# A mixture-of-experts FFN kernel on one core: tile 2's expert mix moved from TensorE to ScalarE and VectorE, buffers and load order around it changed

## The reference, cut to what matters

```python
h = gelu(embedding @ W0 + b0); h = gelu(h @ W1 + b1)
att = softmax(h @ W2 + b2)                              # 32 x 8
agg_w = einsum('bk,koi->boi', att, weight)              # one 128x128 matrix per tile
y = einsum('boi,bih->boh', agg_w, x) + (att @ bias_k)[:, :, None]
# for gate and up, each with its own inv row: scale = max|y * inv| / 127 per row, q = round(y * inv / scale)
gate = (qg @ w_gate.T) * sg * s_wgate                   # 2048 -> 1024
up = (qu @ w_up.T) * su * s_wup
inter = clip(silu(gate) * up, -10, 10)
out = x + (qi @ w_down.T) * si * s_wdown                # quantised again, 1024 -> 2048
```

## Time and profile before

| what | value |
|---|---|
| time, median of 3 runs | 803.78 us (803.5 to 803.93) |
| profiled execution | 803.78 us |
| its span, first to last instruction | 802.0 us |
| around the span | 1.78 us |
| PE busy | 794.1 us (99%) |
| DVE, ACT, POOL busy | 715.4, 441.1, 147.9 us |
| stretch 9 to 56 us, PE idle | 0.47 us of 47 |

### The profile page before, as it was taken

One profiled execution on the slowest core, in us unless ns is written; L12 is line 12 of the kernel. 1 busy time (PEld: TensorE's weight loads), 2 busy tenths in 40 slices (PEclk: granted clock), 3 DMA queues, 4 the chain that ended last, 5 costly groups with the idle time before them and its releaser, 6 DMA issues.

```text
span 802.0 us, 9186 instructions
## 1 busy us (share of the span) xinstructions
PE 794.1 (99%) x3521; PEld 365.3 (46%) x3521; DVE 715.4 (89%) x810; ACT 441.1 (55%) x385; POOL 147.9 (18%) x138
## 2 busy tenths in 40 slices
PE   8999999999999999999999999999999999999997
PEld 5554444444444444444444444444444444444443
DVE  6897899999888998888998888998888988888968
ACT  7774335555664545664545654555654546655531
POOL 2703210210122220122220122210222210222000
PEclk9999999999999999999999999999999999999999
DMA  8998745454445444445444445445455444454342
GB/s 300 225 215 172 161 142 171 149 166 125 131 138 171 145 145 120 129 145 170 145 145 122 119 154 167 147 145 112 122 161 161 154 129 136 108 167 154 90 111 105
DMA packets 162964, 119.81 MB, mean 149 GB/s; under 512 B 151780, under 2 KB 152164, under 8 KB 153703
## 3 DMA queue, kind: packets, MB, share of 16 engines
q1 hardware_dynamic: 161192, 106.64, 44.6%
q0 software_dynamic: 1728, 12.58, 7.8%
HBM read 60.48 MB, written 33.55 MB: 117 GB/s over the span
## 4 chain that ended last, share of the span: by engine, by line
PE 88%; DVE 7%; ACT 2%; issue 1%; DMA 1%; DVEq 0%; ACTq 0%
PE gate_ps L613 26%; PE up_ps L613 25%; PE down_ps L716 22%; PE conv_ps L566 12%; DVE amax L1092 2%; PE gate_ps L716 1%; DVE region L1150 1%; DVE xt L1265 1%; DVE down_sc L1256 1%; ACT qg L820 0%; DMA qgT<-qg 0%; PE up_ps L566 0%; PE down_ps L571 0%; ACT y L809 0%; DVE region L1219 0%
## 5 line engine op out<-in xcount | busy, mean ns | idle before, releaser
L716 PE MATMUL down_ps<-wd,qiT 128*128 128x512 bf16 x896 | 211.2, 379 | 0.0
L613 PE MATMUL gate_ps<-wg,qgT 128*128 128x512 bf16 x928 | 205.7, 379 | 0.0
L613 PE MATMUL up_ps<-wu,quT 128*128 128x512 bf16 x896 | 202.4, 379 | 0.0
L1092 DVE TENSOR_REDUCE amax<-region 128x1 f32<-128x2048 f32 (+1 forms) x90 | 173.0, 1922 | 1.2
L442 POOL TENSOR_TENSOR prod<-wexp,att_bc 128x1024 f32<-128x1024 f32 x28 | 53.1, 1898 | 540.9 <-DVE region L1150 498.3
L716 PEld LDWEIGHTS down_ps<-wd,qiT 128*128 128x128 bf16 x896 | 87.6, 98 | 123.4 <-issue 28.5
L613 PEld LDWEIGHTS gate_ps<-wg,qgT 128*128 128x128 bf16 x928 | 90.8, 98 | 109.4 <-issue 1.1
L613 PEld LDWEIGHTS up_ps<-wu,quT 128*128 128x128 bf16 x896 | 87.7, 98 | 106.1 <-ACT quT L885 0.4
L820 ACT ACTIVATE qg<-region,recip 128x2048 f16<-128x2048 f32 x30 | 60.1, 2002 | 128.9 <-DVE recip L1102 128.9
L566 PE MATMUL conv_ps<-xt,aggw 128*128 128x512 f32 x244 | 116.9, 602 | 0.8 <-ACT y L809 0.5
L809 ACT ACTIVATE y<-conv_ps,aggb 128x512 bf16<-128x512 f32 x116 | 78.9, 686 | 59.6 <-PE conv_ps L566 55.0
(11 more groups left out here) (180 smaller groups left out, 582.1 us busy)
## 6 DMA issues: line engine op xcount, KB each, us to landing
xt<-x SPq DMA_DIRECT2D x30, 1024.0 KB, 4.8
out<-xt SPq DMA_DIRECT2D x29, 1024.0 KB, 4.0
wg<-w_gateT POOLq DMA_DIRECT2D x4, 1024.0 KB, 17.8
wu<-w_upT POOLq DMA_DIRECT2D x4, 1024.0 KB, 15.0
wd<-w_downT POOLq DMA_DIRECT2D x4, 1024.0 KB, 9.6
xt<-x SPq DMA_DIRECT2D x4, 512.0 KB, 4.8
invg_bc<-inv_gate SPq DMA_DIRECT2D x1, 1024.0 KB, 8.2
out<-xt SPq DMA_DIRECT2D x2, 512.0 KB, 2.9
```

The source lines that it names most:

```text
L613: last = nc.tensor.matmul(acc[:, n * BANK:(n + 1) * BANK], codes[:, k * P:(k + 1) * P], wts[:, k, n * BANK:(n + 1) * BANK], start=(k == 0) ...
L716: last = nc.tensor.matmul(down_bank(t, c), qiT_at(t)[:, k * P:(k + 1) * P], wd[:, k, c * BANK:(c + 1) * BANK], start=(k == ks[0]), stop=(k ...
L1092: nc.vector.tensor_reduce(amax[:, i:i + 1], src, axis=AX.X, op=ALU.max, apply_absolute_value=True).then_inc(max_ready, 1)
```

## The change

- Tile 2's mix leaves PE. `experts2` scales the eight experts on ACT, in four pieces between the chunks of `conv_out(0)`, into `prod2`, a part of `wu` that is still empty; `experts2_sum` adds them on DVE in three instructions, put in the middle of tile 0's maxima, into `aggw2`, a part of `qiT`. POOL's up weights wait for it. POOL now writes tile 3's diagonal instead of tile 2's, and `diagonals(3)` on DVE is gone.
- `conv(2)` moves ahead of `turn_g(0)`, `conv(3)` ahead of `turn_g(1)` and of `gate(1)`. Tile 3's `y` is written to `quT`, and its last two chunks use `up_ps`, which `gate(1)` uses too; so `gate(1)` waits for all of `conv_out(3)`.
- ACT's list is rearranged accordingly: `conv_out(2)` between the steps of tile 0, `conv_out(3)` ahead of `turned_g(1)`, `quant_g(2)` ahead of `quant_u(0)`.
- Tile 1's product for up goes to `XU_HOME` in `wd` instead of `region2`; DVE quantises `quant_g(2)` ahead of `quant_u(0)`; tile 3's gate product is made in two halves, one on each side of `gate_out(0)`.
- ACT's queue issues `b2` and `wexp`; SP's list is two issues shorter, and x of tile 3 no longer waits for gate weights. POOL issues the gate weights after x of tile 1 has landed, not x of tile 0.

```diff
...
-Y_HOME = [y[:, :], wd_part(0, bf16), wd_part(1, bf16)]
+Y_HOME = [y[:, :], wd_part(0, bf16), wd_part(1, bf16), quT[:, :]]
 XG_HOME = [region1[:, :], wd[:, :, :].rearrange("p k h -> p (k h)")[:, 6 * H:8 * H].bitcast(fp32)]
...
 def y_at(t):
-    return Y_HOME[t] if t < EARLY else y[:, :]
+    return Y_HOME[t] if t <= EARLY else y[:, :]
...
 def xu_at(t):
-    return XU_HOME if t in (2, EARLY) else region2[:, :]
+    return region2[:, :] if t == 0 or t > EARLY else XU_HOME
...
 ones = qiT[:, 0:2 * P].bitcast(fp32)
+aggw2 = qiT[:, 4 * P:6 * P].bitcast(fp32)
 filler = region1[:, 0:(P + BANK) // 2].bitcast(bf16)
...
 SPLIT = 5
-diag_at = [region2[:, I:H], prod_flat, region2[:, I:H], prod_flat]
+diag_at = {0: region2[:, I:H], EARLY: region2[:, I:H]}
+prod2 = wu[:, 4:6, :].rearrange("p k i -> p (k i)").bitcast(fp32).rearrange("p (k o) -> p k o", o=P)
...
 def conv_bank(t, c):
-    return bank(up_ps, c - 2) if t < EARLY and c >= 2 else bank(conv_ps, c % 2)
+    return bank(up_ps, c - 2) if t <= EARLY and c >= 2 else bank(conv_ps, c % 2)
...
+def aggw_at(t):
+    return aggw2 if t == 2 else aggw[t % 2][:, :]
+
 def xcols(t, c):
...
     sp.dma_start(mlp_s, mlp).then_inc(mlp_in, 16)
-    sp.dma_start(b2_s, b2.partition_broadcast(P)).then_inc(b2_in, 16)
-    sp.dma_start(wexp[:, :, :], weightT).then_inc(wexp_in, 16)
     sp.dma_start(xslot(0), x[0, :, :]).then_inc(x_in[0], 16)
...
         sp.dma_start(swd_s[i], rows[:, (5 + i) * I:(6 + i) * I]).then_inc(rows_in[2 + i], 16)
-    sp.wait_ge(wg_in[0], 16)
     sp.dma_start(xslot(3), x[3, :, :]).then_inc(x_in[3], 16)
...
     pool.wait_ge(att_dve, BIAS[0])
-    a = att_bc[:, 2 * K:3 * K].unsqueeze(2).to_broadcast([P, K, P])
-    nc.gpsimd.tensor_tensor(diag_at[2].rearrange("p (k r) -> p k r", r=P),
+    a = att_bc[:, EARLY * K:FIRST * K].unsqueeze(2).to_broadcast([P, K, P])
+    nc.gpsimd.tensor_tensor(diag_at[EARLY].rearrange("p (k r) -> p k r", r=P),
                             ident[:, :].unsqueeze(1).to_broadcast([P, K, P]), a, ALU.mult).then_inc(diag_pool, 1)
-    pool.wait_ge(x_in[0], 16)
+    pool.wait_ge(x_in[1], 16)
     for i in range(WCH):
...
     pool.wait_ge(row_spread, SWD)
+    pool.wait_ge(sum2, 3)
     for i in range(WCH - 1):
...
             pe.wait_ge(wexp_in, 16)
-        elif t == 2:
-            pe.wait_ge(diag_pool, 1)
         else:
-            pe.wait_ge(diag_dve, 1)
+            pe.wait_ge(diag_pool, 1)
         for k in ks:
...
                 pe.wait_ge(agg_sum, 1)
-            elif t < POOLED:
-                pe.wait_ge(agg_out, t - 1)
+            elif t == 2:
+                pe.wait_ge(sum2, 3)
+            elif t == EARLY:
+                pe.wait_ge(agg_out, 1)
             else:
...
                     pe.wait_ge(logits_out, 1)
-            elif t < EARLY or (t == EARLY and c < 2):
+            elif t <= EARLY:
                 pe.wait_ge(y_ready, NC * t + c - 3)
...
                 pe.wait_ge(y_ready, NC * t + c - 1)
-            nc.tensor.matmul(conv_bank(t, c), aggw[t % 2][:, :], xcols(t, c),
+            nc.tensor.matmul(conv_bank(t, c), aggw_at(t), xcols(t, c),
                              start=True, stop=True).then_inc(conv_done, 1)
...
                 pe.wait_ge(gcodes_ready, 1)
-                pe.wait_ge(agg_out, 2)
+                pe.wait_ge(agg_out, 1)
             turn(gturn_ps[:, h * I:(h + 1) * I], qg, KI, h * KI, gturn_mm)
...
                 pe.wait_ge(qgT_ready, t - EARLY)
-            if t == 0:
-                pe.wait_ge(agg_out, 1)
-            elif t == 1:
-                pe.wait_ge(y_ready, NC * EARLY)
+            if t == 1:
+                pe.wait_ge(y_ready, NC * FIRST)
             elif t == 2 or t == EARLY:
...
     conv(1)
-    aggregate_mm(2)
+    conv(2)
     turn_g(0, range(1))
-    aggregate_mm(3)
+    aggregate_mm(EARLY)
     gate(0, range(4))
     turn_g(0, range(1, 2))
-    conv(2)
+    conv(EARLY)
     turn_g(1)
...
     gate(1, HALVES[0])
-    conv(3)
     gate(0, range(8, 12))
...
                 act.wait_ge(att_dve, BIAS[0])
-            elif t == EARLY:
-                act.wait_ge(xg_ready, 1)
-                act.wait_ge(xu_ready, 1)
             elif t > EARLY:
...
             act.wait_ge(conv_done, NC * t + c + 1)
-            norm = erec[:, t:t + 1] if t < 2 else 1.0
+            norm = erec[:, t:t + 1] if t < EARLY else 1.0
             nc.scalar.activation(y_at(t)[:, c * BANK:(c + 1) * BANK], conv_bank(t, c), ACT.Identity,
...
+    def experts2(ks):
+        for k in ks:
+            nc.scalar.activation(prod2[:, k, :], wexp[:, k, :], ACT.Copy, scale=att_col(2, k)).then_inc(scaled2, 1)
+
     def experts(t):
...
     def aggregate_out(t):
-        act.wait_ge(agg_mm, t)
-        act.wait_ge(conv_done, NC * (t - 1))
+        act.wait_ge(agg_mm, 2)
+        act.wait_ge(conv_done, NC * 2)
         nc.scalar.activation(aggw[t % 2][:, :], agg_ps[t], ACT.Copy, scale=erec[:, t:t + 1]).then_inc(agg_out, 1)
...
             act.wait_ge(row_spread, INVI)
+        elif t == 2:
+            act.wait_ge(xu_ready, FIRST)
         for h in range(2):
...
+    act.dma_start(b2_s, b2.partition_broadcast(P)).then_inc(b2_in, 16)
+    act.dma_start(wexp[:, :, :], weightT).then_inc(wexp_in, 16)
     act.wait_ge(hid_mm, 1)
...
     nc.scalar.activation(group(logits, 1), log_ps[1], ACT.Copy).then_inc(logits_out, 1)
-    conv_out(0)
+    experts2(range(4))
+    conv_out(0, range(1))
+    experts2(range(4, 6))
+    conv_out(0, range(1, 2))
+    experts2(range(6, 7))
+    conv_out(0, range(2, NC))
+    experts2(range(7, K))
     conv_out(1)
+    conv_out(2, range(1))
     quant_g_first(0)
-    aggregate_out(2)
-    turned_g(0, range(1))
+    conv_out(2, range(1, 2))
     quant_g_first(1)
-    aggregate_out(3)
+    turned_g(0, range(1))
+    aggregate_out(EARLY)
+    conv_out(2, range(2, NC))
     turned_g(0, range(1, 2))
     quant_g(1)
-    conv_out(2, range(2))
-    turned_g(1, range(1))
-    conv_out(2, range(2, NC))
-    turned_g(1, range(1, 2))
-    quant_u(0)
-    conv_out(3)
+    conv_out(EARLY)
+    turned_g(1)
     quant_g(2)
+    quant_u(0)
     turned_g(2)
...
-    def diagonals(t):
-        dve.wait_ge(ident_set, 2)
-        dve.wait_ge(agg_sum, 1)
-        a = att_bc[:, t * K:(t + 1) * K].unsqueeze(2).to_broadcast([P, K, P])
-        nc.vector.tensor_tensor(diag_at[t].rearrange("p (k r) -> p k r", r=P),
-                                ident[:, :].unsqueeze(1).to_broadcast([P, K, P]), a, ALU.mult).then_inc(diag_dve, 1)
+    def experts2_sum():
+        dve.wait_ge(scaled2, K)
+        nc.vector.tensor_tensor(prod2[:, 0:4, :], prod2[:, 0:4, :], prod2[:, 4:8, :], ALU.add).then_inc(sum2, 1)
+        dve.wait_ge(sum2, 1)
+        nc.vector.tensor_tensor(prod2[:, 0:2, :], prod2[:, 0:2, :], prod2[:, 2:4, :], ALU.add).then_inc(sum2, 1)
+        dve.wait_ge(sum2, 2)
+        nc.vector.tensor_tensor(aggw2, prod2[:, 0, :], prod2[:, 1, :], ALU.add).then_inc(sum2, 1)
...
         dve.wait_ge(y_ready, NC * t + NC)
-        if t == 2 or t == EARLY:
-            dve.wait_ge(gcodes_ready, 1 if t == 2 else EARLY)
+        if t == 2:
+            dve.wait_ge(gcodes_ready, 1)
         elif t == EARLY + 1:
...
+    def xg_half(t, h):
+        cols = slice(h * I, (h + 1) * I)
+        if h == 0:
+            dve.wait_ge(y_ready, NC * t + NC)
+            dve.wait_ge(gcodes_ready, EARLY)
+        else:
+            dve.wait_ge(part_scaled, NC)
+        nc.vector.tensor_tensor(xg_at(t)[:, cols], y_at(t)[:, cols], invg_bc[:, cols],
+                                ALU.mult).then_inc(xg_ready if h else part_scaled, 1)
+
     def xg_scale(t):
...
             dve.wait_ge(agg_mm, 2)
-        elif t == 2:
+        elif t == 1:
             dve.wait_ge(gcodes_ready, 2)
...
                                     apply_absolute_value=True).then_inc(part_maxed, 1)
+            if c == 1:
+                experts2_sum()
         dve.wait_ge(part_maxed, NC)
...
     quant_first()
-    diagonals(3)
     quant_g(1)
-    quant_u(0)
     quant_g(2)
+    quant_u(0)
     quant_u(1)
-    xg_product(3)
+    xg_half(3, 0)
     gate_out(0)
+    xg_half(3, 1)
     xg_scale(3)```

On PE, from conv of tile 0 to the turn of tile 1; the transposes are the rows of 128x128 from `ident,qg`, the expert mix those from `wexp`. Before:

```order
L566 MATMUL conv_ps<-xt,aggw 128x512 x2
L566 MATMUL up_ps<-xt,aggw 128x512 x2
L566 MATMUL conv_ps<-xt,aggw 128x512 x2
L566 MATMUL up_ps<-xt,aggw 128x512 x2
L537 MATMUL gate_ps<-wexp,region 128x128 x8
L571 MATMUL down_ps<-ident,qg 128x128 x8
L537 MATMUL down_ps<-wexp,prod 128x128 x8
L613 MATMUL gate_ps<-wg,qgT 128x512 x8
L571 MATMUL down_ps<-ident,qg 128x128 x8
L566 MATMUL conv_ps<-xt,aggw 128x512 x2
L566 MATMUL up_ps<-xt,aggw 128x512 x2
L571 MATMUL down_ps<-ident,qg 128x128 x16
```

13 lines of the change are left out of this document (7 added, 6 removed).

## The result

The changed kernel takes 805.41 us in the median of 22 runs (804.80 to 806.86), the kernel before 803.81 us in 22 runs beside them (803.25 to 804.45). The ratio is 1.0020, with a 95% interval of 1.0014 to 1.0026, so 1.1 to 2.1 us slower. The prediction, 803.0 us in a range of 801.9 to 804.2, is wrong, and the sign with it. The profiled execution of the changed kernel took 805.66 us with a span of 803.9, against 802.0 before.

A forecast was written before the change was run, and what follows sets the result against it. PE was taken as the bound, with 88% of the chain. Mix 1.84 plus old waits 0.79, less new waits 0.46, 0.31, 0.34, 0.54 and loads 0.2, gave 0.78 us gain: 803.0 us, range 801.9 to 804.2.

The forecast's parts named there:

- the term on the loads: At the start, mlp shares with ACT's b2 and experts and lands 0 to 0.4 us later; 0.2 taken, all on the path.
- `mlp` at over 2.7 us: Sign at the start: mlp's transfer was expected at 2.3 to 2.7 us; longer would show the forecast wrong.
- Waits 1 to 4: New PE waits: tile 0's first turn 0.46 us, gate(0) 0.31, gate(1) 0.34, turn of tile 3 0.54.
- rival C: DVE's products block on POOL's row spreading, DVE's chain grows another 0.6 to 1.0 us: 803.8, no change; chance 0.12.
- A: Rival: ACT and DVE hand over faster, the first three new PE waits shrink to a third: 802.1; chance 0.13.
- B: Rival: first gate chunk, issued later and behind x of tile 3, lands at 25.7, gate(0) 1.25 us late: 804.2; chance 0.10.
- waits 1 to 3: New PE waits before tile 0's first turn (0.46 us), gate(0) (0.31) and gate(1) (0.34).
- what I don't see in the start: Chance of 0.05 for unforeseen effects at the kernel's start, half of it slower by 0.2% or more.

The follow-up runs named there:

- loads_on_sp: The changed kernel with b2 and the expert weights issued on SP's queue again, behind the small network's weights; 803.49 us, ratio 0.9994 to the kernel before.
- whole_product: loads_on_sp with tile 3's gate product in one piece ahead of gate_out(0) instead of two halves; ratio 1.0001 to the kernel before.
- tile3_first: loads_on_sp with all of tile 3's gate quantising on DVE ahead of gate_out(0), tile 1's and 2's for up behind it; ratio 1.0044 to the kernel before.
- tile3_product_early: tile3_mended with tile 2's product for up moved ahead of gate_out(1) and the remaining attention weights on DVE; 803.95 us, ratio 0.9999 to the kernel before.
- act_after_mlp: The changed kernel with ACT issuing b2 and the experts only after mlp has landed; 812.12 us in one execution.
- tile3_mended_wg: tile3_mended with POOL issuing the gate weights after x of tile 0 has landed, not x of tile 1; ratio 1.0042 to the kernel before.
- tile3_mended: tile3_first with tile 1's product for up back in region2; ratio 1.0038 to the kernel before.

## Why the prediction was wrong

**The step that failed** is the term on the loads: "between 0 and 0.4 us, and I take 0.2, all of it on the path. What could go the other way doesn't count, since neither b2 nor the experts were waited for." Both sentences fell.

- The size. `mlp` lost 0.94 us in the changed kernel, and 1.26 to 1.6 in the others with a load on ACT's queue. 0.4 was no bound from any row, but a guess that a small transfer loses little to others. The prediction itself noted that no row showed two hardware queues at once; then the upper end had to come from the nearest row, which is a large transfer issued behind others: x of tile 0 beside the experts took 6.3 us where its bytes alone take 2.45.
- The experts. They weren't waited for before, but what counts is by how little. In the trace of before they landed at 5.89, and DVE first used them at 6.68: 0.79 us of slack. Putting them in competition with 1 MB of x could take them 2.5 us, its own time, and it did take 2.85. The prediction named the loads in the way of the first gate chunk and worked out their slack, but not here.

The prediction had named `mlp` at over 2.7 us as a sign that it is wrong, and the profile shows 3.2. With 1.87 in place of 0.2, its own sum gives 0.98 - 1.87, a loss of 0.9 us; the measured 1.6 has a further 0.7. In the pair of profiles that is the 0.62 of S - C, whose cause is open, and small terms behind it.

**Waits 1 to 4 held.** Counted from S, since the block moves as one:

| from S, us | predicted | changed kernel |
|---|---|---|
| first turn of tile 0 | 3.89 | 3.81 |
| gate(0) starts | 6.49 | 6.51 |
| gate(1) starts | 15.07 | 15.17 |
| gate(0) ends | 25.53 | 25.59 |
| turn of tile 3 | 32.98 | 33.06 |

Each wait by start-to-start distances: 0.38 (0.46 forecast), 2.25 - 1.84 = 0.41 (0.31), 0.38 (0.34), and before the turn of tile 3 5.75 - 5.18 = 0.57 (0.54). DVE in the changed kernel:

```profile
28.50 3.21 DVE L1122 TENSOR_TENSOR region<-wd,invg_bc 128x2048 f32<-128x2048 bf16 x1 [0.58 <-ACT wd L807]
...
44.72 1.23 DVE L1131 TENSOR_TENSOR region<-quT,invg_bc 128x1024 f32<-128x1024 bf16 x1
46.29 1.28 DVE L1213 SCALAR_TENSOR_TENSOR down_sc<-gate_ps,scale,swg_bc 128x1024 f32<-128x1024 f32 x1 [0.35 <-PE gate_ps L617]
```

The first half is done at 45.95, S + 25.50, where 25.5 to 25.9 was forecast, and `gate_out(0)` waits for PE and not the other way round. One product took 3.21 beside POOL's spreads; so rival C's effect exists, at the size of the earlier trace rows, and not beyond.

**Why the other 1.0 us doesn't show in the medians.** On PE's timeline G - S is 0.79 shorter in the changed kernel and 0.81 in `loads_on_sp`. Yet `loads_on_sp` gains 0.2 in span and in the median. In its profile S - C is 9.21 against 8.51, which took 0.7 of the gain away; C itself was as early as before, and the 0.17 us by which G is ahead is still there when DVE ends. In `whole_product` S - C is 7.88 and G is 0.77 ahead of before; of that 0.34 is lost when PE waits for DVE near 767 us, and 0.4 arrives at the end. So these things stand against a gain of this size: the spread of S - C, 7.6 to 9.2 us in the eight executions whose C is the same to 0.06 us, which the old order absorbs and the new one only in part, and up to 0.6 us in the landing of the last stores. How S - C is spread over the runs that weren't profiled isn't known, so that this is the account of the medians is argued and not shown.

**The rivals.** A (802.1) failed with the loads; waits 1 to 3 didn't shrink. B had the right sign, but not the place: the first gate chunk, issued at 13.62 instead of 11.74, took 10.6 us and landed at 24.2, 0.4 behind the forecast 23.8, and gate(0), late by itself, didn't wait for it. But the slack is as thin as B feared: in `tile3_first` and `tile3_product_early`, where conv was quick, gate(0) waited 0.8 us for this chunk. The 0.05 for "what I don't see in the start", half of it slower, was where the result lay. It should have had far more, as the one part of the change for which no row of before gave a bound.

## What to carry to other kernels

A load on which the first chain of work depends should have its moment alone: here anything else issued on another hardware queue at the same time, even 4 KB, cost it about a microsecond or more. "Not waited for" is no reason to leave a load out of the sum; subtract landing from first use, and compare that slack with the full time of the transfer that newly stands beside it. And in a hand-written order, a product that frees a buffer for a later load is on the path too, though the wait shows 30 us later and on another engine.

## What the runs showed of the hardware

- **Two queues at once.** `mlp`, 153 KB, lands 2.2 to 2.4 us after its issue where nothing is issued on ACT's queue until then, in nine profiled executions, and 3.2 to 3.9 us in the five where something is. The Trainium skill, "DMA: Bandwidth & Descriptors", section "Issuing engines are not separate DMA queues", says that transfers of all issuing engines share the DMA engines and that a second issuing engine saves only the time of issuing. The runs agree that there is no gain; they show a cost of 0.9 to 1.6 us for the first transfer.
- **Shares.** The experts' 0.5 MB took 4.1 to 4.9 us on SP's queue ahead of x, and 7.3 to 7.6 on ACT's queue beside it. Meanwhile DMA moved 408 GB/s in the changed kernel from 4 to 8 us and 407 in `loads_on_sp`: the same bytes in another order. The Trainium skill, "DMA: Bandwidth & Descriptors", section "Queues, rings and completion order", says that an engine takes turns between queues, a packet at a time. The runs agree in this: a transfer that is done early when it stands ahead of x in one queue shares with x from another. A small transfer can be slow as well: `b2`, 4 KB, took 8.1 us in `act_after_mlp`.
- **PE's first passes.** Passes of conv are 0.85 us apart at first and 0.43 later, while the granted clock is shown as 1.00, the level of 2.4 GHz, in both stretches. The change-over came at 12.8 us in the first profile of before, ahead of 11.9 in the second, and near 15.7 in the changed kernel. In `tile3_mended_wg` passes of conv(3) are 0.86 us apart at a granted clock of 0.50, so the first passes go at the pace of that level although the granted clock doesn't show it. This is worth 0.9 us between two executions of one kernel and up to 1.6 between executions with the same C, as much as the whole change; why it varies is open.
- **A wait can lower the clock.** PE stood still for 2.2 us before conv(3) in `tile3_mended_wg` and for 4.2 before the down product in `tile3_product_early`; behind both the granted clock read 0.50, the level of 1.2 GHz, and PE lost 1.7 and 1.3 us on top of the wait. Behind waits of 2.2 and 2.0 us in `tile3_first` and `tile3_mended` it stayed at 1.00.
